# Recurrent layers: the first norm's chunk sums move from TensorE to POOL, and its variance, rstd, scaling and affine move later

## The reference, cut to what matters

```
xa  = layernorm(x) * ln1_w + ln1_b              # the "first norm"
sx  = previous token's xa - xa
xxx = tanh((xa + sx * maa_x) @ maa_w1)          # 5 small projections, each 32 wide
xm  = xa + sx * (maa_stack + xxx_j @ maa_w2_j)  # j = k, w, v, r, g
w   = exp(-exp(time_decay + tanh(xw @ td_w1) @ td_w2))
r, k, v, g = xr @ Wr.T, xk @ Wk.T, xv @ Wv.T, silu(xg @ Wg.T)
for every token: a = k v^T (per head 16 x 16); out = r (u a + s); s = a + w s
og  = norm per head of out, * gn_w + gn_b
x1  = x + (og * g) @ Wo.T
xc  = layernorm(x1)...; x1 + sigmoid(xr2 @ Wfr.T) * (relu(xk2 @ Wfk.T)^2 @ Wfv.T)
```

## Time and profile before

| | |
|---|---|
| median of 3 runs | 3028.55 us (3027.71 to 3029.18) |
| profiled execution | 3034.8 us, its span 3033.0 us |
| PE busy in the span | 2794.6 us (92%) |
| DVE | 2018.6 us (67%) |
| ACT | 1338.9 us (44%) |
| POOL | 666.1 us (22%), 436 instructions |
| first recurrent layer | about 592 to 1295 us of the span |
| second recurrent layer | about 2314 us to the end |

### The profile page before, as it was taken

The page is one execution under the profiler, slowest core; times in us unless marked ns, Lnnn a source line. Parts: engine busy times, 40 slices in busy tenths (PEclk is TensorE's granted clock), DMA queues, the critical chain, the costliest instruction groups (busy, mean ns, idle before and its releaser), DMA issues.

```text
span 3033.0 us, 53535 instructions
## 1 busy us (share of the span) xinstructions
PE 2794.6 (92%) x18016; PEld 2174.6 (72%) x18016; DVE 2018.6 (67%) x4921; ACT 1338.9 (44%) x3438; POOL 666.1 (22%) x436
## 2 busy tenths in 40 slices
PE   7999999978999999689999999999997889999986
PEld 7555555766888888585455545899996768888866
DVE  2878787678999999654555555410101799999992
ACT  1888888543444443343444444323211234444432
POOL 0011110034444444200000000000000444444440
PEclk9999999988999999899999999999997889999998
DMA  2101010323333333200000000300002333333340
GB/s 108 37 24 35 23 35 13 132 77 94 90 92 87 93 87 94 89 28 20 21 29 20 20 20 10 153 1 1 0 1 90 107 92 91 91 89 90 93 126 11
DMA packets 96168, 182.86 MB, mean 60 GB/s; under 512 B 10122, under 2 KB 87498, under 8 KB 92462
## 3 DMA queue, kind: packets, MB, share of 16 engines
q1 hardware_dynamic: 96046, 181.27, 19.3%
HBM read 171.34 MB, written 9.90 MB: 60 GB/s over the span
## 4 chain that ended last, share of the span: by engine, by line
PE 66%; DVE 13%; issue 10%; ACT 8%; POOL 1%; DMA 1%; DVEq 0%; SPq 0%; ACTq 0%; POOLq 0%
PE psum L529 20%; PE psum L318 10%; PE psum L2000 6%; PE psum L1887 4%; PE psum L1362 3%; DVE psum L739 3%; PE psum L520 3%; ACT arena L1647 3%; ACT arena L2255 2%; PE psum L1900 2%; PE psum L1942 2%; PE psum L536 2%; PE psum L1374 2%; DVE arena L754 2%; PE psum L1341 2%
## 5 line engine op out<-in xcount | busy, mean ns | idle before, releaser
L529 PE MATMUL psum<-arena 128*128 128x200 f32 x4096 | 777.9, 349 | 52.3 <-DVE arena L920 18.6
L529 PEld LDWEIGHTS psum<-arena 128*128 128x128 f32 x4096 | 727.6, 199 | 136.5 <-issue 79.6
L1163 POOL TENSOR_TENSOR arena<-arena 128x800 f32<-128x800 f32 x256 | 454.7, 1779 | 456.6 <-DVE psum L739 456.6
L754 DVE TENSOR_TENSOR_SCAN arena<-arena,psum 128x808 f32<-128x808 f32 x256 | 470.0, 1836 | 40.1 <-PE psum L520 24.9
L318 PE MATMUL psum<-arena 128*128 128x200 f32 (+1 forms) x1920 | 332.8, 335 | 15.1 <-POOLq L140 13.4
L318 PEld LDWEIGHTS psum<-arena 128*128 128x128 f32 x1920 | 328.6, 192 | 17.5 <-POOLq L140 13.4
L1647 ACT ACTIVATE arena<-arena 100x361 f32<-100x361 f32 x512 | 300.5, 590 | 86.7 <-DVE arena L1574 85.0
L1143 POOL TENSOR_TENSOR arena<-arena 128x800 f32<-128x800 f32 x80 | 141.7, 1771 | 773.9 <-DVE arena L762 526.9
L1574 DVE CUSTOM_DVE_ANT_0 arena<-psum,arena 100x361 f32<-100x361 f32 x512 | 254.2, 530 | 45.5 <-ACT arena L1647 37.9
L739 DVE TENSOR_TENSOR psum<-arena 128x808 f32<-128x808 f32 x256 | 280.0, 1094 | 5.6
L1362 PEld LDWEIGHTS psum<-arena 100*128 100x128 f32 x1536 | 145.9, 141 | 131.3 <-ACT arena L1659 60.3
(11 more groups left out here) (143 smaller groups left out, 3853.0 us busy)
## 6 DMA issues: line engine op xcount, KB each, us to landing
arena<-v_rows SPq DMA_DIRECT2D x512, 202.0 KB, 3.2
arena<-ctxT SPq DMA_DIRECT2D x32, 722.0 KB, 4.2
arena<-L_w SPq DMA_DIRECT2D x9, 1024.0 KB, 10.5
arena<-L_w SPq DMA_DIRECT2D x8, 1152.0 KB, 16.1
v_rows<-arena SPq DMA_DIRECT2D x32, 202.0 KB, 2.0
arena<-L_fc SPq DMA_DIRECT2D x4, 1024.0 KB, 7.8
arena<-L_pj SPq DMA_DIRECT2D x4, 1024.0 KB, 15.7
arena<-xT SPq DMA_DIRECT2D x4, 800.0 KB, 12.2
```

The costliest lines, as they stand in the source:

```text
L529: mm = pe.matmul(chunk(bank, j), m.W[n][:, k, c * P:(c + 1) * P], src[:, k, :], start=k == 0, stop=k == C - 1)
L754: dve.tensor_tensor_scan(m.ring[n % 4].rearrange("p j e -> p (j e)"), m.we[:, cc].rearrange("p j e -> p (j e)"), m.kv, 0.0, ALU.mult, ALU. ...
L1163: pool.tensor_tensor(sv, sv, rb, ALU.mult).then_inc(sem("r_states"), 1)
```

## The change

POOL gets two pairs of adds per turn (`add_chunks`): chunks 0 and 1 plus chunks 2 and 3 (128 x 400), and the two halves of that (128 x 200), with a wait on its own semaphore between them. One pair sums the squares of group g+1, behind the product of item 1 (n == 2 in POOL's list). The other sums X of group g+2, a turn ahead, behind the product of item 7 (n == 8), into a buffer of its own, `fold`. PE then needs one matmul in place of four for each average, and waits for `folded`. Its variance matmul moves from before the reduction of items 14 and 15 to just before the second half of k. On ACT the squares of the norm per head come first, Ln of the first norm behind them, Exp of it behind the Ln of the norm per head, and its affine part behind the evictions of k and r, before `start(7)`. On DVE the scaling moves from behind item 2 to behind item 4 and the multiplication of the norm per head. The loop has turns 2 to 5, and turn 6 is written out, since its POOL has no group g+2 to sum. The load of the constants tells the signal of the input's rest in place of one of its own; every engine that waited for one waited for both.

```diff
-        self.input_rest = self.new_signal("input_rest", 48)
-        self.constants = self.new_signal("constants", 16)
+        self.input_rest = self.new_signal("input_rest", 64)
...
+        self.fold = r.take(N)
...
-        with eng.Fori(2, G - 1) as g:
+        with eng.Fori(2, G - 2) as g:
             body(g + base, g, front=True, rec=True, back=True, tail=True)
+        body(base + G - 2, G - 2, front=True, rec=True, back=True, tail=True)
...
 # PE
-                m.n1.pe_mean(pe, lambda c: X[:, c, ds(g + 1, N)], f)
+                wait(pe, "folded", f, 2)
+                pe.matmul(m.n1.mean_ps, core.mean_w, m.fold, start=True, stop=True).then_inc(m.n1.mu.sem, 1)
...
-            if front:
-                m.n1.pe_var(pe, f)
-                if not rec and after.tail:
+            def front_var():
+
+                wait(pe, "folded", f, 4)
+                pe.matmul(m.n1.var_ps, core.mean_w, m.n1.s2[:, 0], start=True, stop=True).then_inc(m.n1.var.sem, 1)
+
+            if front and not rec:
+                front_var()
+                if after.tail:
...
                 else:
                     wait(pe, "v", i, 1)
+                if front:
+                    front_var()
                 project_half("k", m.xm[0], 1, 2, "k_sum")
...
 # DVE: from behind item 2 to behind item 4
-            if front:
-                m.n1.scale(dve, f)
-                rest(1, dve, "squares 2", front, rec)
...
                 dve.tensor_tensor(m.oc, m.oc, m.ors, ALU.mult).then_inc(sem("head_normed"), 1)
                 ahead(1, dve, "centre", rec, back)
+            if front:
+                m.n1.scale(dve, f)
+                rest(1, dve, "squares 2", front, rec)
...
 # ACT, part 4
-                m.n1.act_rstd(act, f)
-                rest(2, act, "squares 2", front, rec)
...
                 act.activation(m.osq, m.oc, ACT.Square).then_inc(sem("head_squares"), 1)
+            if front:
+                act.wait_ge(m.n1.var.sem, m.n1.var.at(f, 1))
+                act.activation(m.n1.rs, m.n1.var_ps, ACT.Ln, bias=core.epsc[:, 0:1]).then_inc(m.n1.lnv.sem, 1)
...
 # ACT, part 5: the affine part goes, Exp comes between Ln and Exp of the heads
                 act.activation(two(m.ors), wide[2], ACT.Ln, bias=core.epsc[:, 0:1]).then_inc(sem("head_log_var"), 1)
+            if front:
+                act.wait_ge(m.n1.lnv.sem, m.n1.lnv.at(f, 1))
+                act.activation(m.n1.rs, m.n1.rs, ACT.Exp, scale=-0.5).then_inc(m.n1.rstd.sem, 1)
+                rest(2, act, "squares 2", front, rec)
+            if back:
                 wait(act, "head_log_var", b, 1)
...
 # ACT, behind the evictions of k and r (part 6), before start(7)
+            if front:
+                m.n1.wait_scaled(act, f)
+                if rec:
+                    wait(act, "mixed", i, 5)
+                for c in range(C):
+                    act.activation(m.xs[:, c, :, 1:E], seq(m.n1.yc)[:, c], ACT.Identity, bias=vec("ln1_b", c),
+                                   scale=vec("ln1_w", c)).then_inc(sem("xa"), 1)
+                rest(2, act, "rstd 2", front, rec)
...
 # POOL
+            def add_chunks(a, k, out, j, n):
+                pool.tensor_tensor(a[:, 0:2], k[:, 0:2], k[:, 2:4], ALU.add).then_inc(sem("folded"), 1)
+                wait(pool, "folded", j, n)
+                pool.tensor_tensor(out, a[:, 0], a[:, 1], ALU.add).then_inc(sem("folded"), 1)
+
+            if front and not rec:
+                pool.wait_ge(m.n1.mu.sem, m.n1.mu.at(f))
+                add_chunks(m.n1.yc, xg(g + 1), m.fold, f, 1)
             for n in range(16):
+                if front and n == 2:
+                    pool.wait_ge(m.n1.sq.sem, m.n1.sq.at(f, 1))
+                    add_chunks(m.n1.s2, m.n1.s2, m.n1.s2[:, 0], f, 3)
+                if front and n == 8 and not (isinstance(g, int) and g + 2 >= G):
+                    if rec:
+                        wait(pool, "bonus_sum", i, 1)
+                    else:
+                        wait(pool, "xa", f, 4)
+                    pool.wait_ge(m.n1.mu.sem, m.n1.mu.at(f, 1))
+                    add_chunks(m.n1.yc, xg(g + 2), m.fold, f + 1, 1)
```

More of the change, by code:

```diff
@@ L111, in load @@
             if q == 1:
-                sp.dma_start(self.arena[:, C * T:self.own], self.dram["const"]).then_inc(self.constants.sem, 16)
+                sp.dma_start(self.arena[:, C * T:self.own], self.dram["const"]).then_inc(self.input_rest.sem, 16)
     def load_weights(self, sp, after, spans, source, told):
@@ L148, in wait_before @@
             eng.wait_ge(self.input_rest.sem, self.input_rest.at(1))
-            eng.wait_ge(self.constants.sem, self.constants.at(1))
 class Layer:
@@ L337 @@
     state0_in_xs2=1, xc=4, shift2=1, ffn_mix=8, ffn_k_sum=2, ffn_relu=2, ffn_squared=2, ffn_r_sum=2, ffn_tanh=2,
-    ffn_v_sum=2, ffn_gated=2, group_done=1)
+    ffn_v_sum=2, ffn_gated=2, group_done=1, folded=4)
 BACK = DM * 2
@@ L1005, in body @@
                 act.activation(m.osq, m.oc, ACT.Square).then_inc(sem("head_squares"), 1)
+            if front:
+                act.wait_ge(m.n1.var.sem, m.n1.var.at(f, 1))
+                act.activation(m.n1.rs, m.n1.var_ps, ACT.Ln, bias=core.epsc[:, 0:1]).then_inc(m.n1.lnv.sem, 1)
             start(5)
-            if front:
-                m.n1.wait_scaled(act, f)
-                if rec:
-                    wait(act, "mixed", i, 5)
-                for c in range(C):
-                    act.activation(m.xs[:, c, :, 1:E], seq(m.n1.yc)[:, c], ACT.Identity, bias=vec("ln1_b", c),
-                                   scale=vec("ln1_w", c)).then_inc(sem("xa"), 1)
-                rest(2, act, "rstd 2", front, rec)
             if back:
```

## The result

The kernel after takes 3047.28 us (median of 4 runs, 3046.93 to 3049.23), the kernel before 3028.13 beside it (4 runs): 1.0069 times as long, 95% interval 1.0056 to 1.0082. The forecast was 3035.5, its range ended at 3044. The change made the kernel 19 us slower by the medians, 2.7 times the +7 forecast.

What follows compares the result with a forecast made beforehand. PE and DVE, both nearly fully busy, were taken to share the bound of each turn. Turn 0 +8.4, turn 1 -0.6, regular turns -1.8, fill +0.95 made +7 us on 3028.55: 3035.5, range 3025 to 3044.

Steps and rivals of the forecast that it cites:

- Turn 0: Turn 0 of each layer: PE waits for POOL's adds, DVE enters item 7 3.8 us late; together +8.4.
- Failed step 1: Regular turn without a dip: DVE loses 0.6 us at the gate (late tanh), 0.45 hidden, so turn 0.15 longer.
- Failed step 2: Regular turns after a clock dip: 0.54 us gained on PE, 0.4 at the residual add.
- Turn 1: Turn 1: PE's half-clock variance leaves the start, late eviction takes most back; -0.3 us each, -0.6.
- The two adds: POOL's adds of squares behind item 1: 0.855 and 0.48 us, 0.07 between, 1.4 in all before PE's variance.
- The frame: Loop of one turn less, that turn written out, and the constants' signal merged: cost 0.
- Fill: Turn -1: POOL's adds for group 1 get in DVE's way, +1.2 us each; both layers together +0.95.
- (a): Rival: PE is the bound, POOL's adds hidden; -13 us in twelve turns, 3024 with turn 0's cost; chance 0.13.
- (b): Rival: idle PE's granted clock falls before k, 1.5 us in each of ten regular turns, 3050; chance 0.12.
- (c): Rival: clock dips vanish as turn length changes, eight of 0.9 us = -7, so 3028.5; chance 0.12.
- (d): Rival: v's eviction isn't the decider in turn 0, which costs 2.3 us a layer: 3031.5; chance 0.18.
- The three signs by which I said I would be wrong: k starts before 4.4 us behind product 2; turn 0 grows under 2 us; PE's clock falls before k.

Runs made afterwards that it cites:

- g4: Kernel after without POOL's adds of squares, variance taken from chunk 0 alone (another value, only time read): 3031.18 us, 1.0018 of before.
- f2: Kernel after with turn 0's variance on PE moved behind the second halves of k and r: 3047.09 us, 1.0057 of before.
- h1f3: Kernel after with v's second half evicted between the two affine parts and turn 0's variance behind k's half only: 3032.78 us, 1.0022 of before.
- h1: Kernel after with v's second half evicted between the affine part of n1 and that of the heads: 3041.01 us, 1.0044 of before.
- f12: Kernel after with v's second half evicted ahead of n1's affine and turn 0's variance behind k and r: 3042.84 us, 1.0050 of before.
- f1: Kernel after with v's second half evicted ahead of the affine of n1: 3058.34 us, 1.0100 of before.
- g1: Kernel before with only the moves on DVE and ACT; sums and variance on PE as before: 3042.86 us, 1.0055 of before.
- e1_after: Kernel after, unchanged, measured and profiled once more: 3046.98 us, 1.0072 of before.
- g3: Kernel before with only the mean moved (POOL sums chunks a turn ahead, PE one matmul) and the change's whole frame: 3027.67 us, 1.0008 of before.
- k0: Kernel before with only the frame: loop one turn shorter, turn 6 written out, constants' signal merged: 3032.41 us, 1.0017 of before.
- k1: Kernel before with only the constants' signal merged: 3026.75 us, 0.9995 of before.
- k2: Kernel before with only the loop one turn shorter and turn 6 written out on all four engines: 3032.12 us, 1.0007 of before.
- m1: Kernel before with only the mean moved to POOL's sums a turn ahead, turn 6 written out for POOL alone: 3029.32 us, 1.0002 of before.
- m2: Kernel after with v's eviction between the affine parts, turn 0's variance behind k's half, turn 6 written out for POOL alone: 3038.09 us, 1.0033 of before.

## Why the prediction was wrong

**Turn 0: right in size, in part by luck.** +8.4 forecast, +8.6 in both executions. The first links are in the rows: variance 6.8 us later, a slow k, DVE's idle before item 4, and g4 (without the adds) gives it all back. But the forecast had DVE only 2.3 late at item 4 and let the late eviction of v bring it to 3.8. It was 3.6 late at ruk already (5.0 in the second layer), ahead of any wait for tanh: item 4's scan came 2.9 and 4.4 late, and the scaling, which now stands behind it, adds 0.7. The gate then added 0.4 (1.1), not all of which lasted. So by the traces the decider in turn 0 was PE's first reduction, and not the eviction; no run takes the eviction's path alone out of turn 0. The variance's place alone takes out 2.6 (f2 against after), 4.7 (h1f3 against h1) and 11.6 (f12 against f1).

**Failed step 1: "DVE loses 0.6. Of that the 0.45 us that it waited at 835.67 hides all but 0.15."** The gate came 1.8 late, not 0.6. The eviction of v was 2.62 later, not 1.85: the adds took 0.3 longer and product 2 came 0.35 later, so k's half was late, the heads' variance behind it too (rstd 0.23 earlier than before and not 0.93), and DVE waited 0.44 for the reduction of item 4, which the forecast did not have; its 0.81 for rstd it had. Item 5 was to start within 0.1 us of before, and ruk behind it came 0.65 late. The DMA's way out and back took 6.44 instead of 6.07, another 0.4. And the cushion of 0.45 was none: what ended that wait is PE's output projection, and PE waits for the same gate (0.38 at 830.27, the first half of the projection) and for DVE's bonus behind the gate (0.64 at 833.86, ahead of the second half). A late gate moves PE and DVE together, and 0.45 stands unchanged at 838.53. What shows it: h1 (turns 2 to 6 from +6.1 to +1.1 by one eviction, nine of ten waits of the gate gone) and g1 (the gate's wait without any adds). The four turns that followed no dip before were forecast at +0.6 and came out at +4.6 (5.7 in e1_after).

**Failed step 2: "such a turn gains 0.54 on PE and 0.4 at the residual add."** k's half in a turn after a dip came 4.99 behind product 2 and not 4.6: 0.16 gained, not 0.54, and the late gate took more than that. The six turns were forecast at -2.4 and came out at +1.6 (-0.1 in e1_after). As a mechanism the gain exists: in g3, where nothing else is late, the turns that follow a dip and dip themselves are 0.5 to 0.8 shorter.

Together these make +5.9 (6.1 and 5.6) where -1.8 was forecast, 7.7 us of the 12 by which the time was missed. **Turn 1** has the same path; -0.6 forecast, and between -0.6 and +3.3 by execution and reference: not settled.

**The two adds.** The small one was put at 0.48, between two rows; measured 0.61. The large one took 1.03 where a 128x400 in another stage had taken 0.855, which is the larger part of the miss. The page of the Trainium skill weighed there ("GPSIMD Engine Reference", section 3.1) was nearer for the small add: an estimate by its fixed part gave 0.58. The "about 1 us later" that this would have made of the sum is far less than the 12 us that were missing. The rows 1.74, 1.03 and 0.61 for 800, 400 and 200 elements lie near a line with about 0.25 us at zero, an estimate of mine in which the first row is a product and the others are adds.

**The frame**, forecast at 0, measured at +2 to +8 us (k0), with its parts at -5 to +2 (k1) and -1 to +6 (k2). The argument, from the chain through the loop's edge, held for the turns; that k0 is longer than before has no cause shown.

**Fill**, +0.95 forecast: the collision is as described, but the start of turn 0 lies between 639.8 and 647.7 in executions of kernels that measure the same, so its sum cannot be read.

**The time of the profile.** I forecast the profiled execution 6.3 us over the median, as it was for before: 3041.8. It took 3047.14, 0.1 below its median. The distance of one profiled execution from its median did not carry over. The forecast of the median does not rest on it, but the 12.3 by which after's span exceeds that of before would have hidden 7 us of the loss; against k1, profiled near its median, it is 19.6.

**Rivals.** (a) fell: PE was not the bound; in turn 2 of g3 1.0 us less on PE was worth 0.01. (b) fell: at 1.4 us of idle before k the clock stayed full in every regular turn, though its number, 3050, was nearest. (c) came true and helped nothing: 5 or 6 of 8 dips vanished, and the undipped turn was as long as the dipped one of before. (d) had the better mechanism for turn 0 (DVE at item 4, not the eviction) with a price too low: 2.3 a layer, where DVE was 3.6 and 5.0 late before any wait for tanh. Its number for the whole, 3031.5, was far off. The three signs by which I said I would be wrong all came out in favour of the forecast; none of them looked at item 7, where the gate is. Those of the signs of being right that looked there did not hold: start column 8 came 3.0 later and not 1.9, and DVE waited 1.19 for tanh and not 0.6.

**Open.** g3 and m1 gain 5 us in turns 2 to 6, and do not measure faster. In their profiles the stretch between the two layers is 4 to 5 us longer than in k1. It varies from 1174.6 to 1180.5 over the kernels, above 1178 in g1, g3, k0, k2, m1 and m2 and below in all others; whether this is the place of the code, the arrival of the weights or chance was not settled. Of the 2.8 us of the 19.6 that lie outside the turns, 0.5 is in this stretch; none of the 2.8 has a cause shown.

## What to carry to other kernels

A wait that will hide a loss is a cushion only if its releaser does not depend on the thing that is late: follow the releaser back before counting it. When an instruction is moved on an in-order queue, list what is behind it and go to the longest way out of there (here an eviction with a DMA out and back, 6 us ahead of a gate), since a POOL sum that takes 1.0 us off the matrix engine can put 1.7 us in front of everything behind it. And test one half alone: the half that ran a turn ahead (the mean, g3) gained in its turns, though not in the measured time, and the half in line (the variance) lost.

## What the runs showed of the hardware

- An add of 128x200 on POOL took 0.61 us, one of 128x400 1.03, and a product of 128x800 1.74: by a line through these three, splitting a sum into small steps costs about 0.25 us a step, an estimate. A 128x400 add in another stage took 0.855, so the stage matters too.
- POOL and DVE, both on SBUF operands, excluded each other in small operations too. In the fill DVE's subtraction started at 604.71, 0.03 behind POOL's add, and ended at 606.57, 0.85 behind the end of that add: 1.86 instead of 0.99. POOL's next add started at 605.80 and ended 0.47 behind the subtraction: 1.24 instead of 0.61.
- The granted clock fell to its lower level in v's half after 1.14 us of idle (1010.46, mean 0.63), and stayed full (1.00) at the variance and k's half after 1.40 (807.54). The same idle gives either, as it did in before at 1005.80 and 849.96.
- Executions of one kernel spread over 15 us (before: 3021.6 to 3036.9 in 32 runs). Two profiles of before differ by up to 2.5 us in turns 0 and 1 and by 0.14 in turns 2 to 6, each; two of after by up to 3.0, and by up to 0.94 in turns 2 to 6, where a dip comes or stays away.
